# Normalising feed-forward rows two steps ahead, and scoring layer 1's first pair among the last feed-forward steps

## The chip, the cores and the metric

One NeuronCore of one Trainium2 chip runs the whole program. The metric is device time in microseconds (us), the median of several executions. The engines are TensorE (PE in the views, PEld for its weight loads), VectorE (DVE), ScalarE (ACT), GpSimd (POOL) and the sync engine (SP), which issues the DMAs inside the attention layers. Each engine works through its own instruction stream in order and waits on semaphores where it needs another's result.

## The reference

The input x is 64 sequences of 64 channels by 256 positions, float32. It goes through four blocks, each added to x:

```
x = x + L0_xattn(layernorm(x), ctx)   # banded attention (|i-j| <= 64), 8 heads, relu gate, mix
x = x + L0_ffn(layernorm(x))          # out = (x @ weight) * scale, then a norm rule on each row:
                                      #   out *= tanh(n) / (n + 1e-7), out *= min(0.99 / |out|, 1)
x = x + L1_xattn(layernorm(x), ctx)   # full attention, 8 heads, rotary q and k
x = x + L1_ffn(layernorm(x))          # 4-bit weights with low-rank terms, relu, 256 -> 1024 -> 256
```

Both attentions need softmax over exp(score - row maximum), so a pair's row maxima come before its exponentials. A row of the layer-0 feed-forward is 256 values in and out; its sum of squares gives n.

## The kernel before

X stays in on-chip memory as 32 pairs of sequences, [128, 32, 256]. Everything runs pair by pair.

**Attention.** One `iteration(r)` of a layer works on several pairs at once, 16 heads each: it scores pair r+1 (`score_head`, TensorE line 451) for its row maxima (`maximum`, VectorE line 1157), forms the shifted scores of pair r (`shifted_head`, line 467) for the exponentials (`exp_head`, ScalarE line 757), and projects q and k of pair r+3. In layer 1 a projection (line 503) is followed by the rotary rows: ScalarE copies them with halves swapped (`turn_rows`, line 786, two activations each for q and k), VectorE multiplies (`rotate`, line 1185), GpSimd adds (`rot_sum`, lines 1368 and 1373), ScalarE rounds the high part (`high_part`, line 774) and GpSimd forms the two lower parts (`split`, lines 1353 to 1360). SP then lays the parts out and replicates them (`lay_out`, lines 359 and 362, `replicate`, lines 373 and 375); `score_head` waits for all of it on `stack_in`. GpSimd splits the row maxima (`split_max`, lines 1022 and 1024), TensorE turns them (`turn_max`, line 543), ScalarE copies them out (`max_out`, line 812), and SP writes them into the stacked rows (`shift_rows`, line 384), for which `shifted_head` waits. Iterations -3, -2 and -1 only fill this pipeline.

**Layer-0 feed-forward.** It has 36 steps, written out by hand. In step n VectorE normalises row pair n (`vector_apply` into `ff0_xn`, line 1132; the views call it ff_xn) and keeps the result of n-4 (`tensor_copy` into `ff`, line 1276). TensorE transposes pair n (line 658) and multiplies pair n-2 (line 672). ScalarE copies the transpose out (`ff0_xT`, line 939) and squares the product of n-2 with an accumulated sum (`junk`, line 945). Four product banks (1, 5, 3, 4) and two transpose banks (0, 2) are used in turn. Steps 0 to 7 stand beside the heads of layer 0's last iteration (`ff0_filling`). Steps 8 to 35 follow in `ff0_steps`, which calls `between(n)` ahead of each step. This `between` is each engine's list of what else is done there:

- the tail of layer 0's attention (n = 8 to 16);
- the feed-forward's gains for the first six pairs: `root` and `tanh` on ScalarE, `gain_norm` and `gain_clip` on VectorE (lines 1081 to 1102), six times `ff0_update` (line 1072 and the statistics in line 1029) at n = 12 to 14, the variance at n = 15, `vector_rstd` and the first `apply` of layer 1 at n = 17;
- layer 1's iteration -3 (TensorE n = 18, ScalarE 19 and 22, VectorE 20) and -2 (TensorE 23 and 30, ScalarE 24 and 31, VectorE 25), cut by heads.

After step 35 TensorE waits until VectorE has kept all 32 results (`f_keep`), because layer 1 scores into banks 0, 1 and 5 and its exponentials use 2 and 3. Only then does `run(-1)` start with iteration -1. VectorE does the gains of the other 26 pairs inside iteration -1 (`vector_within`) and updates X with them in iterations 0 to 9, two to five pairs in each.

The GpSimd and SP streams have no `between`: they start on layer 1 when layer 0 is done and wait for what they need. For SP the order in an iteration is side load, layout of pair r+2, maxima of pair r (second half), replication of pair r+2, maxima of pair r+1 (first half).

Of the kernel before, what the change touches and what calls it, by code (L numbers as in the profile page):

```python
# [15 lines left out]
PAIRS = BATCH // 2  # L16
HPP = 2 * HEADS
# [12 lines left out]
EARLY = PAIRS // X_CHUNKS  # L30
FF0_RING = 4
FF0_LAG = (2, 2, 4)
FIRST_CHUNK, SECOND_CHUNK = 6, 16
FILL = 8
SCORE_BANKS = 3
# [45 lines left out]
def build(nc, a, out):  # L81
# [12 lines left out]
    with stack:  # L94
# [186 lines left out]

        def ff0_turn_bank(n):

            return bank[2 if n > FILL and n % 2 else 0], n if n <= FILL else n - 1

        def ff0_bank(n):

            if n < FILL:
                return bank[(1, 5)[n % 2]], n - 1
            return bank[(1, 5, 3, 4)[n % 4]], n - 1 if n < FILL + 2 else n - FF0_RING + 1  # L290


# [348 lines left out]
        def _(e):  # L641
# [38 lines left out]
            def between(n):  # L680
                if n - FILL in tail:
                    tail[n - FILL]()
                if n == 18:
                    iteration(*early(-3))
                if n == 23:
                    iteration(*early(-2, range(0, 6)))
                if n == 30:
                    iteration(*early(-2, range(6, HPP)))

            ff0_steps(ff0, between)  # L690
            e.wait_ge(f_keep, PAIRS)
            run(-1)
            tail = next_tail

            def turn_chunk(c, cu):
# [222 lines left out]
        @block.scalar  # L918
        def _(e):
            e.dma_start(lora_in, a["lora_in"]).then_inc(lora_loaded, 16)  # L920
            e.dma_start(lora_out, a["lora_out"]).then_inc(lora_loaded, 16)
            e.dma_start(att_w[1][:, :, :], a["att_w1"]).then_inc(weights1_in, 16)
            e.dma_start(att_b[1][:, :], a["att_b1"]).then_inc(weights1_in, 16)
            e.wait_ge(cleared_s, 1)
            nc.scalar.activation(gain[:, 0:1], gain[:, 0:1], ACT.Sqrt).then_inc(table_in, 1)
            e.wait_ge(cleared_k, 1)
            e.dma_start(Ks[SHIFT_ROW:SHIFT_ROW + PARTS, :, :, :].rearrange("p a h t -> p (a h t)")
                        .bitcast(fp32), a["minus"]).then_inc(minus_in, 16)
            scalar_prepare(e, -AHEAD - 1)
            e.wait_ge(ln_var, 1)  # L930
            scalar_sqrt(0, EARLY)
            e.wait_ge(weights0_in, 2 * 16)

            def ff0(pair):
                n, u = num(pair, FF0_RING), pair[1]
                if active(pair, FF0_RING):
                    e.wait_ge(f_xT, n + 1)
                    wait_some(e, f_mm, n - FF0_RING + 1)
                    nc.scalar.activation(ff0_xT[:, u, :], ff0_turn_bank(n)[0][:, 0:T], ACT.Copy).then_inc(f_xTs, 1)
                late = at(pair, -FF0_LAG[1], FF0_RING)  # L940
                n, u = num(late, FF0_RING), late[1]
                if active(late, FF0_RING):
                    e.wait_ge(f_mm, n + 1)
                    wait_some(e, f_sq, n - 1)
                    nc.scalar.activation(junk[:, u % 2, :], ff0_bank(n)[0][:, 0:T], ACT.Square,
                                         accum_out=sumsq[:, bass.ds(n, 1)]).then_inc(f_sq, 1)

            _, run, tail = scalar_attention(e, 0, scalar_prepare, ff0_filling(ff0))
            run(-AHEAD)

            def root(chunk, first, end):
                e.wait_ge(f_sq, end)
                nc.scalar.activation(tmp[:, 0, first:end], sumsq[:, first:end], ACT.Sqrt).then_inc(f_root, 1)

            def tanh(chunk, first, end):
                e.wait_ge(f_norm, chunk + 1)
                nc.scalar.activation(tmp[:, 2, first:end], tmp[:, 1, first:end], ACT.Tanh).then_inc(f_tanh, 1)

            iteration, run, next_tail = scalar_attention(e, 1, scalar_edges)

            def between(n):
                if n - FILL in tail:
                    tail[n - FILL]()
                if n == 8:
                    root(0, 0, FIRST_CHUNK)
                if n == 10:
                    tanh(0, 0, FIRST_CHUNK)
                if n == 16:
                    e.wait_ge(ln_var, 4)
                    scalar_sqrt(0, FIRST_CHUNK)  # L970
                if n == 19:
                    iteration(*early(-3, range(0, 6)))
                if n == 22:
                    iteration(*early(-3, range(6, HPP)))
                if n == 24:
                    iteration(*early(-2, range(0, 6)))
                if n == 25:
                    e.wait_ge(ln_var, 5)
                    scalar_sqrt(TAIL_NORM, PAIRS)
                if n == 31:  # L980
                    iteration(*early(-2, range(6, HPP)))

            ff0_steps(ff0, between)
            root(1, FIRST_CHUNK, PAIRS)
            tanh(1, FIRST_CHUNK, PAIRS)
            run(-1, loop_from=4)
            tail = next_tail

            def turn_out(c, cu):
                e.wait_ge(g_xT, CHUNK * c + CHUNK)  # L990
                wait_some(e, g_up, HB * c - HB)
                for blk in range(2):
                    nc.scalar.activation(xT[:, cu, blk, :], bank[blk][:, :], ACT.Copy).then_inc(g_xTs, 1)

            def relu_chunk(c, cu, beside={}):
                wait_some(e, g_down, CHUNK * c - CHUNK)
                for hb in range(HB):
                    if hb in beside:
                        beside[hb]()
                    e.wait_ge(g_up, HB * c + hb + 1)  # L1000
                    nc.scalar.activation(hidden[cu][:, hb, :], bank[2 + hb % 2][:, :], ACT.Relu,  # L1001
                                         bias=up_b[:, hb:hb + 1]).then_inc(g_relu, 1)

            turn_out(0, 0)
            relu_chunk(0, 0, tail)
            turn_out(1, 1)
            e.wait_ge(ln_var, 9)
            scalar_sqrt(TAIL_NORM, PAIRS)
            relu_chunk(1, 1)
            with e.Fori(1, PAIRS // CHUNK // 2) as i:  # L1010
                turn_out(i * 2, 0)
                relu_chunk(i * 2, 0)
                turn_out(i * 2 + 1, 1)
                relu_chunk(i * 2 + 1, 1)
# [90 lines left out]
        def vector_within(e, n, h):  # L1105


            if n == -1 and h == 2:
                gain_norm(e, 1, FIRST_CHUNK, PAIRS)
            if n == -1 and h == 6:  # L1110
                gain_clip(e, 1, FIRST_CHUNK, PAIRS)
            if n in (0, 1) and h % 3 == 1 and h < 15:
                ff0_update(e, FIRST_CHUNK + 5 * n + h // 3)
            if n == 1 and h == 15:
                vector_var(e, FIRST_CHUNK, SECOND_CHUNK, ff_vec, SECOND_CHUNK + NORM_STEPS)
            if n == 2 and h == 1:
                vector_rstd(e, 6, FIRST_CHUNK, SECOND_CHUNK)
            if 2 <= n < 10 and h in (3, 11):
                ff0_update(e, SECOND_CHUNK + 2 * (n - 2) + h // 8)
            if n == 9 and h == 15:  # L1120
                vector_var(e, SECOND_CHUNK, PAIRS, ff_vec, PAIRS + 2 * NORM_STEPS)
            if n == 10 and h == 1:
                vector_rstd(e, 7, SECOND_CHUNK, PAIRS)
# [11 lines left out]
        def vector_attention(e, l, extra=None, within=None, beside=None):  # L1135
# [81 lines left out]
            if l == 0:  # L1217
                tail[6] = lambda: update(at(TAIL, -1))

            def iteration(r):  # L1220
                p1, p3, m1 = at(r, 1), at(r, AHEAD), at(r, -1)
                for h in range(HPP):
                    if within and isinstance(r[0], int):
                        within(e, num(r), h)
                    if h == 5:
# [29 lines left out]
        def _(e):  # L1255
# [7 lines left out]
            e.wait_ge(weights0_in, 2 * 16)  # L1263

            def ff0(pair):
                n, u = num(pair, FF0_RING), pair[1]
                if n == 0:
                    e.wait_ge(ffn_ready, PREP_BLOCKS)
                if active(pair, FF0_RING):
                    wait_some(e, f_xT, n - FF0_RING + 1)  # L1270
                    vector_apply(n, ff0_xn[:, u, :], f_xn)
                late = at(pair, -FF0_LAG[2], FF0_RING)
                n, u = num(late, FF0_RING), late[1]
                if active(late, FF0_RING):
# [10 lines left out]
            def between(n):  # L1285
# [15 lines left out]
                    iteration(*early(-3)[:1])  # L1301
                if n == 21:
                    vector_var(e, TAIL_NORM, PAIRS, ln_vec, PAIRS + NORM_STEPS)
                if n == 28:
                    vector_rstd(e, 5, TAIL_NORM, PAIRS)
                if n == 25:
                    iteration(*early(-2)[:1])

            ff0_steps(ff0, between)
            e.wait_ge(f_keep, PAIRS)  # L1310
            run(-1, loop_from=4)
            tail = next_tail

            def norm_chunk(c):
# [232 lines left out]
```

## Time and profile before

| | |
|---|---|
| median of 3 runs | 1329.06 us (1322.9 to 1331.28) |
| the profiled execution | 1333.56 us |
| its span, first to last instruction | 1331.8 us |
| mean granted TensorE clock | 0.982 of full speed |
| TensorE busy | 1263.2 us (95%) |
| VectorE busy | 909.1 us (68%) |
| ScalarE busy | 847.8 us (64%) |
| GpSimd busy | 676.6 us (51%) |

The profiled execution took 4.5 us more than the median of the runs. Times inside the span are counted from its first instruction. A row of a timeline gives start, duration, engine, line, operation and, in brackets, how long the engine had been idle and who released it. The granted clock is 1.00 at TensorE's upper level (2.4 GHz) and 0.50 at the lower (1.2 GHz).

### The profile page before, as it was taken

How to read it: one execution, taken by the hardware profiler on the slowest of the kernel's cores; microseconds unless marked ns; L12 is line 12 of the kernel's file. 1: busy time of each engine (PE TensorE's matmuls, PEld its weight loads, DVE VectorE, ACT ScalarE, POOL GpSimd, SP SyncE). 2: the span in 40 equal slices, each digit the busy share in tenths (PEclk: the TensorE clock that was granted, in tenths of full speed). 3: DMA queues.
4: the chain of work that ended last, by engine and by line, in shares of the span. 5: the costliest groups of instructions: out<-in, count | busy, mean ns of one | idle time of the engine just before them, and what ended most of it. 6: DMA issues, size and time to landing. Idle time of an engine off the chain costs nothing.

```text
span 1331.8 us, 35495 instructions
## 1 busy us (share of the span) xinstructions
PE 1263.2 (95%) x11100; PEld 839.9 (63%) x11100; DVE 909.1 (68%) x1924; ACT 847.8 (64%) x1849; POOL 676.6 (51%) x1169
## 2 busy tenths in 40 slices
PE   6999999999999998778899999999999989999998
PEld 3666667667776765454565656666666546666665
DVE  6778778888887875569999978888888842111110
ACT  2567677776777776556888788888888763222111
POOL 4577778787878865045455445555555211000000
PEclk9999999999999999888999999999999999999999
DMA  8554454544444440034344434444444300000000
GB/s 206 120 131 107 114 117 111 116 110 118 113 114 117 99 92 7 13 67 102 89 107 96 97 90 103 105 112 97 103 108 108 86 2 16 16 16 16 16 16 32
DMA packets 90486, 113.34 MB, mean 85 GB/s; under 512 B 13971, under 2 KB 80275, under 8 KB 82739
## 3 DMA queue, kind: packets, MB, share of 16 engines
q1 hardware_dynamic: 89216, 111.25, 35.9%
q10 hardware_dynamic: 1206, 1.29, 0.3%
q8 instruction: 34, 0.56, 0.2%
q14 instruction: 30, 0.25, 0.1%
HBM read 18.66 MB, written 4.19 MB: 17 GB/s over the span
## 4 chain that ended last, share of the span: by engine, by line
PE 73%; DVE 10%; POOL 6%; issue 4%; ACT 3%; DMA 2%; SPq 1%; POOLq 0%; ACTq 0%; DVEq 0%
PE bank L491 13%; PE bank L451 12%; PE bank L467 12%; PE bank L721 8%; PE bank L712 8%; PE bank L449 5%; DVE row_max L1157 5%; PE bank L503 4%; POOL probs L1386 4%; PE bank L672 2%; PE bank L522 2%; PE bank L555 2%; PE bank L532 1%; PE bank L543 1%; DVE stats L1029 1%
## 5 line engine op out<-in xcount | busy, mean ns | idle before, releaser
L1157 DVE TENSOR_REDUCE row_max<-bank 128x2 f32<-128x384 f32 (+1 forms) x1024 | 598.5, 617 | 107.0 <-PE bank L451 102.8
L757 ACT ACTIVATE probs<-bank 128x384 f32<-128x384 f32 (+1 forms) x1024 | 536.8, 542 | 165.1 <-PE bank L467 154.8
L451 PE MATMUL bank<-Ks,Qs 96*128 96x192 bf16 (+1 forms) x2048 | 371.4, 263 | 10.9 <-DVE row_max L1157 9.7
L467 PE MATMUL bank<-Qs,Ks 128*128 128x192 bf16 (+1 forms) x2048 | 366.3, 261 | 13.9 <-ACT probs L757 11.1
L1386 POOL TENSOR_SCALAR_AFFINE_SELECT probs<-probs 128x256 f32<-128x256 f32 (+1 forms) x512 | 259.1, 530 | 105.9 <-ACT probs L757 85.5
L451 PEld LDWEIGHTS bank<-Ks,Qs 96*128 96x128 bf16 x2048 | 186.4, 98 | 121.1 <-DVE row_max L1157 39.7
L491 PE MATMUL bank<-probs,V 128*32 128x192 f32 (+1 forms) x4096 | 248.0, 360 | 4.7 <-POOL probs L1386 3.4
L467 PEld LDWEIGHTS bank<-Qs,Ks 128*128 128x128 bf16 x2048 | 186.7, 98 | 45.4 <-ACT probs L757 28.7
L449 PE MATMUL bank<-band,ident 128*128 128x384 bf16 x512 | 168.8, 330 | 2.5 <-DMA Ks<-Ks 2.0
L491 PEld LDWEIGHTS bank<-probs,V 128*32 128x32 f32 x4096 | 107.3, 109 | 84.5 <-issue 40.5
L1323 DVE TENSOR_TENSOR X<-bank,X 128x256 f32 (+1 forms) x32 | 13.6, 425 | 185.6 <-PE bank L721 185.6
L712 PE MATMUL bank<-Ks,ffn_w 128*128 128x512 f32 x256 | 111.8, 593 | 0.0
L1459 POOL TENSOR_TENSOR X<-X,down_b 128x256 f32 x32 | 23.1, 750 | 169.5 <-DVE xn L1132 169.5
L1368 POOL TENSOR_TENSOR rot<-rot,rope 128x256 f32<-128x256 f32 x64 | 46.7, 730 | 117.7 <-ACT rot L786 117.7
L712 PEld LDWEIGHTS bank<-Ks,ffn_w 128*128 128x128 f32 x256 | 48.4, 190 | 56.8 <-issue 56.4
L1001 ACT ACTIVATE probs<-bank,up_b 128x512 f32<-128x512 f32 x32 | 22.0, 687 | 85.7 <-PE bank L712 85.7
L1001 ACT ACTIVATE Qs<-bank,up_b 128x512 f32<-128x512 f32 x32 | 22.0, 687 | 76.1 <-PE bank L712 76.1
L449 PEld LDWEIGHTS bank<-band,ident 128*128 128x128 bf16 x512 | 49.4, 96 | 32.0 <-issue 15.6
L1357 POOL TENSOR_SCALAR Qp<-q_rest 128x256 bf16<-128x256 f32 x64 | 54.3, 848 | 27.3 <-DVE q_rest L1167 21.9
L503 PE MATMUL bank<-xn,att_w 128*128 128x256 f32 x192 | 63.9, 418 | 1.8 <-DVE xn L1132 1.6
L1022 POOL TENSOR_TENSOR row_max<-row_max 128x16 f32<-128x16 f32 x64 | 13.8, 215 | 100.7 <-DVE row_max L1157 100.7
L786 ACT ACTIVATE rot<-bank,att_b 64x256 f32<-64x256 f32 x128 | 60.0, 469 | 3.4 <-PE bank L503 0.3
(114 smaller groups left out, 1625.2 us busy)
## 6 DMA issues: line engine op xcount, KB each, us to landing
Ks<-Ks SPq DMA_DIRECT2D x64, 576.0 KB
Qs<-Qs SPq DMA_DIRECT2D x128, 192.0 KB
Qs<-Qp SPq DMA_DIRECT2D x192, 64.0 KB
Ks<-Kp SPq DMA_DIRECT2D x192, 64.0 KB
X<-in_x SPq DMA_DIRECT2D x4, 1024.0 KB, 13.8
side<-in_ctx_crossed SPq DMA_DIRECT2D x32, 128.0 KB, 2.1
side<-in_ctx SPq DMA_DIRECT2D x32, 128.0 KB, 2.1
out<-X SPq DMA_DIRECT2D x8, 512.0 KB, 3.0
```

Source lines behind the costliest of these rows:

```text
L449: nc.tensor.matmul(dst[:, 0:2 * win], ident16[:, :], band16[:, :], start=True, stop=False)
L451: last = nc.tensor.matmul(dst[:, blk * win:(blk + 1) * win], Qs[0:SHIFT_ROW, pair[1], h, blk * P:(blk + 1) * P], Ks[0:SHIFT_ROW, pair[1], ...
L467: last = nc.tensor.matmul(dst[:, blk * win:(blk + 1) * win], Ks[:, pair[1], h, blk * P:(blk + 1) * P], Qs[:, pair[1], h, start(blk):start( ...
L491: last = nc.tensor.matmul(dst[32 * j:32 * j + 32, first:first + win], V[:, pair[1], column:column + 32], probs[:, head % 8, blk * win:(blk ...
L503: nc.tensor.matmul(job_bank[b][:, 0:T], w[:, weight, :], source, start=True, stop=True).then_inc(s[f"{b}_filled"], 1)
L712: last = nc.tensor.matmul(bank[2 + hb % 2][:, :], up_w[:, blk, hb * P:(hb + 1) * P], xT[:, cu, blk, :], start=(blk == 0), stop=(blk == 1))
L721: last = nc.tensor.matmul(bank[4 + j % 2][:, 0:T], hidden[cu][:, hb, j * P:(j + 1) * P], down_w[:, hb, :], start=(hb == 0), stop=(hb == HB ...
L757: nc.scalar.activation(probs[:, h % 8, 0:2 * win], exp_bank[h % 2][:, 0:2 * win], ACT.Exp, scale=SCALE).then_inc(s["exped"], 1)
L786: nc.scalar.activation(rot[here, 2 * n + 1, :], job_bank[bk][there, 0:T], ACT.Identity, bias=b[there, column:column + 1]).then_inc(s["turn ...
L1157: nc.vector.tensor_reduce(row_max[:, pair[1], h // HEADS, 0, h % HEADS * 2:h % HEADS * 2 + 2], bank_of(pair, h)[:, 0:2 * win].rearrange("p ...
L1357: nc.gpsimd.tensor_scalar(parts[:, u, 1, :], rest[:, :], 1.0, None, ALU.mult).then_inc(s[mid], 1)
L1386: return nc.gpsimd.affine_select(out=part, in_=part, compare_op=ALU.is_ge, fill=0.0, base=base, pattern=[[0, 4], [-sign, width]], channel_ ...
```

## The change

VectorE's part of the feed-forward runs two row pairs ahead: step 0 normalises pairs 0, 1 and 2, and step n pair n+2. The four buffers of `ff0_xn` are the same, so step n waits for the transpose of pair n-2 in place of n-4. The reciprocal for the last four pairs moves from n = 28 to n = 26, and ScalarE's square root for it from n = 25 to n = 23.

From pair 28 on the feed-forward uses three banks in place of six: transposes only bank 2, products banks 3 and 4 in turn. Banks 0, 1 and 5 are so free for scores. TensorE scores heads 0 to 2 of layer 1's pair 0 ahead of step 32 and heads 3 and 4 ahead of step 33, with the projection of pair 2's q at head 1; the rest of iteration -1 follows step 35, ahead of the wait for `f_keep`. VectorE takes maxima 0 and 1 ahead of step 33, 2 to 4 ahead of step 34 and 5 to 7 ahead of step 35, and the rest after the steps. ScalarE's part of iteration -1 follows its steps, with `tanh` in the middle of it, and VectorE's gains move from heads 2 and 6 to heads 8 and 14. GpSimd and SP are unchanged.

```diff
+FF0_LATE = 28
+FF0_AHEAD = 2
...
         def ff0_turn_bank(n):
 
+            if n >= FF0_LATE:
+                return bank[2], n
             return bank[2 if n > FILL and n % 2 else 0], n if n <= FILL else n - 1
...
                 return bank[(1, 5)[n % 2]], n - 1
+            if n >= FF0_LATE:
+                return bank[(3, 4)[n % 2]], n - 1
             return bank[(1, 5, 3, 4)[n % 4]], n - 1 if n < FILL + 2 else n - FF0_RING + 1
...
                     iteration(*early(-2, range(6, HPP)))
+                if n == 32:
+                    e.wait_ge(f_xTs, FF0_LATE)
+                    e.wait_ge(f_keep, FF0_LATE - 2)
+                    iteration(*early(-1, range(0, 3)))
+                if n == 33:
+                    iteration(*early(-1, range(3, 5)))
 
             ff0_steps(ff0, between)
+            iteration(*early(-1, range(5, HPP)))
             e.wait_ge(f_keep, PAIRS)
-            run(-1)
+            run(0)
...
-                if n == 25:
+                if n == 23:
                     e.wait_ge(ln_var, 5)
                     scalar_sqrt(TAIL_NORM, PAIRS)
...
             root(1, FIRST_CHUNK, PAIRS)
+            iteration(*early(-1, range(0, 9)))
             tanh(1, FIRST_CHUNK, PAIRS)
-            run(-1, loop_from=4)
+            iteration(*early(-1, range(9, HPP)))
+            run(0, loop_from=4)
...
-            if n == -1 and h == 2:
+            if n == -1 and h == 8:
                 gain_norm(e, 1, FIRST_CHUNK, PAIRS)
-            if n == -1 and h == 6:
+            if n == -1 and h == 14:
                 gain_clip(e, 1, FIRST_CHUNK, PAIRS)
...
             def ff0(pair):
-                n, u = num(pair, FF0_RING), pair[1]
+                n = num(pair, FF0_RING)
                 if n == 0:
                     e.wait_ge(ffn_ready, PREP_BLOCKS)
-                if active(pair, FF0_RING):
-                    wait_some(e, f_xT, n - FF0_RING + 1)
-                    vector_apply(n, ff0_xn[:, u, :], f_xn)
+                for step in range(FF0_AHEAD + 1) if n == 0 else (n + FF0_AHEAD,):
+                    if step < PAIRS:
+                        wait_some(e, f_xT, step - FF0_RING + 1)
+                        vector_apply(step, ff0_xn[:, step % FF0_RING, :], f_xn)
...
-                if n == 28:
+                if n == TAIL_NORM - FF0_AHEAD:
                     vector_rstd(e, 5, TAIL_NORM, PAIRS)
                 if n == 25:
                     iteration(*early(-2)[:1])
+                if n == 33:
+                    iteration(*early(-1, range(0, 2)))
+                if n == 34:
+                    iteration(*early(-1, range(2, 5)))
+                if n == 35:
+                    iteration(*early(-1, range(5, 8)))
 
             ff0_steps(ff0, between)
+            iteration(*early(-1, range(8, HPP)))
             e.wait_ge(f_keep, PAIRS)
-            run(-1, loop_from=4)
+            run(0, loop_from=4)
```

## Rows read from the trace of the kernel before

**Rows 1.** Busy time by stretch: window, us, PE, PEld, DVE, ACT, POOL, PEclk, DMA share, GB/s
```profile
534.00:563.00 29.00, 21.77 (x101) 14.62 (x94) 17.80 (x58) 13.04 (x40) 0.72 (x1) 0.82 0.05 14
563.00:592.00 29.00, 22.19 (x95) 17.70 (x93) 15.35 (x41) 16.86 (x59) 12.39 (x18) 0.82 0.25 53
592.00:608.00 16.00, 11.51 (x49) 5.19 (x50) 14.94 (x31) 5.60 (x13) 10.13 (x17) 0.65 0.47 104
...
900.00:1000.00 100.00, 99.83 (x1001) 64.82 (x1005) 86.40 (x158) 85.49 (x186) 53.88 (x95) 1.00 0.45 104
```

**Rows 2.** TensorE's waits, 534 to 592 us: us in total, times, longest
```profile
PE bank L658 <- DVE ff_xn L1132: 13.6, 6, 3.2
```

**Rows 3.** Timeline, all engines, around step 20
```profile
563.12 1.03 PE L672 MATMUL bank<-ff_w,ff_xT 128*128 128x256 f32 x4
...
563.60 1.95 ACT L786 ACTIVATE rot<-bank,att_b 64x256 f32<-64x256 f32 x4
...
566.37 0.81 DVE L1132 TENSOR_SCALAR ff_xn<-X,mean,rstd 128x256 f32<-128x256 f32 x1
...
567.17 0.72 POOL L1373 TENSOR_TENSOR k_rest<-rot 128x256 f32<-128x256 f32 x1
...
567.23 0.69 PE L658 MATMUL bank<-ident,ff_xn 128*128 128x128 f32 x2 [3.08 <-DVE ff_xn L1132]
...
567.71 1.91 PE L672 MATMUL bank<-ff_w,ff_xT 128*128 128x256 f32 x4
```

**Rows 4.** TensorE's timeline, an undisturbed step (27 and 28), and two windows
```profile
583.70 0.38 PE L658 MATMUL bank<-ident,ff_xn 128*128 128x128 f32 x2
583.91 1.03 PE L672 MATMUL bank<-ff_w,ff_xT 128*128 128x256 f32 x4
584.78 0.38 PE L658 MATMUL bank<-ident,ff_xn 128*128 128x128 f32 x2
...
567.00:573.00 6.00, 5.77 (x17) 4.66 (x18) 3.96 (x16) 2.40 (x9) 1.10 (x3) 0.50 0.01 1
...
580.00:583.00 3.00, 3.00 (x10) 2.44 (x10) 1.54 (x5) 1.18 (x4) 0.45 (x1) 0.50 0.79 152
```

**Rows 5.** VectorE's timeline, steps 11 to 17
```profile
540.36 0.41 DVE L1132 TENSOR_SCALAR ff_xn<-X,mean,rstd 128x256 f32<-128x256 f32 x1
...
541.02 0.47 DVE L1072 SCALAR_TENSOR_TENSOR X<-ff,gain,X 128x256 f32<-128x256 f32 x1
...
542.72 0.40 DVE L1132 TENSOR_SCALAR ff_xn<-X,mean,rstd 128x256 f32<-128x256 f32 x1
...
558.80 0.18 DVE L1051 RECIPROCAL rstd<-rstd 128x6 f32<-128x6 f32 x1
```

**Rows 6.** TensorE's timeline, steps 2 and 5 in layer 0's last iteration
```profile
518.12 0.45 PE L658 MATMUL bank<-ident,ff_xn 128*128 128x128 f32 x2 [1.07 <-DVE ff_xn L1132]
...
527.15 0.44 PE L658 MATMUL bank<-ident,ff_xn 128*128 128x128 f32 x2 [0.31 <-DVE ff_xn L1132]
```

**Rows 7.** Pair 0's way to its stacked rows: timeline of ACT and SP, one window
```profile
572.17 0.41 ACT L774 ACTIVATE Qp<-q_rest 128x256 bf16<-128x256 f32 x1
...
582.40 0.82 SPq L375 DMA_DIRECT2D Ks<-Ks  x1
...
587.00:588.00 1.00, 1.00 (x9) 0.97 (x8) 0.66 (x2) 0.66 (x3) 0.00 (x0) 1.00 0.39 82
```

**Rows 8.** Timeline, iteration -1: TensorE, ScalarE and VectorE
```profile
592.53 0.39 PE L451 MATMUL bank<-Ks,Qs 96*128 96x256 bf16 x2 [1.02 <-DVE ff L1276]
...
594.69 1.95 ACT L786 ACTIVATE rot<-bank,att_b 64x256 f32<-64x256 f32 x4
...
600.96 6.66 DVE L1157 TENSOR_REDUCE row_max<-bank 128x2 f32<-128x512 f32 x11
607.54 0.48 DVE L1072 SCALAR_TENSOR_TENSOR X<-ff,gain,X 128x256 f32<-128x256 f32 x1
```

More of the change, by code:

```diff
@@ L1218, in vector_attention, with iteration @@
                 tail[6] = lambda: update(at(TAIL, -1))
-            def iteration(r):
+            def iteration(r, heads=range(HPP)):
                 p1, p3, m1 = at(r, 1), at(r, AHEAD), at(r, -1)
-                for h in range(HPP):
+                for h in heads:
                     if within and isinstance(r[0], int):
```

## The prediction

> **What bounds the kernel now.** I read the table by stretch first. In layer 1's steady state TensorE is busy 99.83 of 100 us; in the feed-forward steps it is busy 21.8 of 29 us and again 22.2 of 29, at a mean granted clock of 0.82 [rows 1]. So the stretch from 534 to 592 us loses time in two ways. The list of TensorE's waits names the first: 13.6 us in six waits, all of the transposes for a normalised row pair [rows 2]. The timeline shows how one arises. At step 20 ScalarE spends 1.95 us on the rotary rows, VectorE waits for them, and only then normalises pair 20; TensorE has nothing from 564.15 to 567.23, 3.08 us [rows 3]. The second loss follows the first: after the wait the four matmuls of a product take 1.91 us in place of 1.03, and the window 567 to 573 has a granted clock of 0.50, the lower of the two levels [rows 3, 4]. An undisturbed step takes 1.08 us (transpose to transpose) [rows 4].
>
> From 592.5 on VectorE bounds: 14.94 of 16 us busy [rows 1], with layer 1's first score at 592.53 and the last maximum of pair 0 ending just before 607.54, 15.0 us later [rows 8]. From there the work is the same before and after the change, so I take 607.54 as the point to compare.
>
> **Part 1, two steps ahead.** It adds and removes no instruction, only the places change; the three first normalisations stand together in step 0, where TensorE needs only the first. The work by stage, with times as in this execution:
>
> *Layer 0's last iteration.* The waits of steps 2 and 5 (1.07 and 0.31 us [rows 6]) go, since those pairs were normalised earlier. I count 1.2.
>
> *Steps 8 to 17.* VectorE does its gains up to 540.36. From there it has work without a pause: six pairs of normalisation and copy (540.36 to 541.02, 0.66 each), six updates with statistics (541.02 to 542.72 is two, 0.85 each), two updates of layer 0's tail at the same 0.85, and seven small operations for the variance, some 0.8 [rows 5]. That is 3.9 + 5.1 + 1.7 + 0.8 = 11.5 us, so the reciprocal that was at 558.80 comes at about 551.9: 6.9 earlier. TensorE no longer sits behind it step by step: it may be two steps on. It needs 1.08 a step and some 2 us for the tail, under 9 us in all, so VectorE bounds here, not TensorE. TensorE's and ScalarE's earlier lag goes too: q and k of pair 0 are projected at about 552.5, and after steps 18 and 19 of 1.08 us ScalarE's rotary rows start at about 555.1 in place of 563.60 [rows 3], 8.5 earlier.
>
> *Steps 19 to 22.* The stall of 3.08 us shrinks to what ScalarE's 1.95 us leave, about 0.9, and the lower clock behind it (three steps at 2.1 in place of 1.08) goes. GpSimd's last sum for pair 0 ends 4.3 us after the rotary rows start (563.60 to 567.89 [rows 3]), so at 559.4. ScalarE's high part of q, which waited at 572.17 for its turn in the steps [rows 7], comes at about 559.1: 13.0 earlier.
>
> *Steps 23 to 31.* The stall ahead of step 25 goes the same way, with its lower clock (580 to 583 at 0.50 [rows 4]). With step 22 at 558.5, ten steps of 1.08, the projections (0.9 and 0.4) and 0.8 for ScalarE's rows TensorE is at step 32 at about 571.5.
>
> **Part 2, the early scores.** They need pair 0's stacked rows. Before, the last copy was issued at 582.40 and the transfers ran on to about 587.9 (82 GB/s still in the window to 588, of which the last part is mine to divide from the side load) [rows 7], 15.7 us after the high part. Nothing in that chain (GpSimd, SP, four dependent transfers) is changed, so it lands at T = 559.1 + 15.7 = 574.8. TensorE stands at step 32 from 571.5 and waits 3.3 us there, with products 30 and 31 queued behind the first score.
>
> Behind T the order costs something. VectorE's early maxima include the rotation of pair 2's q ahead of step 34, and ScalarE does those rows only after square 31 and `root`. At the lower level, which followed idle times of 3.08 and 3.24 us [rows 3, 4], three heads (0.43 each, twice the full-speed 0.2 per head of rows 8) and a projection (0.86) end at T + 2.2; a product is 0.86 at full speed, what a step of 1.08 leaves beside its transpose [rows 4], and 1.7 at half. Product 30 ends at 3.6, with the clock back on the way, heads 3 and 4 at 4.05, product 31 at 4.9, its square at 5.5, the root at 5.8, q's two rows (0.98 [rows 8]) at 6.75, and VectorE rotates at T + 6.85. It had finished maxima 0 to 2 and one copy at T + 3.55, so it waits 3.3 us. Its remaining work is that of before, 15.0 us from first score to last maximum [rows 8], and three copies that now lie within it, 1.0. The last maximum ends at T + 15.0 + 1.0 + 3.3 = T + 19.3 = 594.1, 13.5 us ahead of 607.5. With the 1.2 of the opening that is 14.7.
>
> Without part 2 the scores would start at the same T and end at T + 15.0, so I price part 2 by itself at +4.3 us. The bounds: -2 if the rows land early enough that maxima run beside the products, +6 if the clock stays low through both products.
>
> *Costs that no row shows.* The three banks: a late product waits for the copy of the one two before it. The cost lies between 0 and a whole step of 1.08 us for each of four steps, 4.3; I take 0, because the 3.3 us wait for T covers most of it. A normalisation beside GpSimd's work takes 0.81 in place of 0.41 [rows 3, 5]; VectorE has room where that happens, so between -0.5 and +1; I take 0. The clock between 541 and 552 us: TensorE has gaps of 1 to 1.5 us there, shorter than the ones that preceded a fall, but many. A fall would cost up to 2 us behind VectorE's bound; I take 1.0. The moved square root loads no table and the gains only trade places: 0.
>
> Sum: 14.7 - 1.0 = 13.7 us. The profiled execution, 1333.56, would become 1319.9; on the median, 4.5 lower, 1329.1 - 13.7 = **1315.4**.
>
> [...]
>
> **Rivals.** (a) *The early scores are free.* The rows land by 572 to 573, or TensorE comes late enough to find them there, and the maxima fill VectorE's gaps. Then part 2 costs nothing and part 1 gives its whole 19.0 less 1.0: 1329.1 - 18 = 1311. For it: VectorE is idle about half of steps 24 to 31 (15.35 busy of 29 [rows 1]). Against: T follows from the high part by a chain that I see at 15.7 us, and everything that TensorE gains makes it arrive earlier before T.
>
> (b) *Half the gain.* TensorE's waits for normalised rows are replaced by waits for VectorE's kept results or ScalarE's copies: both engines do the same 1.95 us of rotary rows, tanh and root in the same places. If each of the six waits keeps half its length and its lower clock, half of the 13.0 stays: 7.7 in all with the opening, less 1.0: 1322.4. For it: each wait in rows 2 has another busy engine behind it. Against: four buffers and banks let TensorE run two steps on.
>
> (c) *Slower.* The waits are cut into many short gaps, and the clock stays at the lower level through the steps. From step 13 (541.3) 19 steps at 2.14 us make 40.7, tail, projections and V at half speed 6.8; TensorE comes to step 32 at 588.8, where it was at about 589.5. Part 1 then gives 0.7 + 1.2 = 1.9, and part 2 costs its 4.3: 2.4 slower, 1331.5. It decides from the point where part 1 saves less than 4.3. Against it: from 583 to 589 the clock is full with this very pattern of steps.
>
> (d) *The ahead does not happen where it matters*, since the wait for the transpose of n-2 binds VectorE: then a pair is normalised one step ahead at most. TensorE transposes n-2 two steps before it is needed, so I see nothing for it; it would end near (b).
>
> **How the numbers follow.** My forecast 0.45, (a) 0.2, (b) with (d) 0.28, (c) 0.07. The range goes from 1306, a little under (a), to 1326, over (b), which leaves out (c) and the far ends. One per cent, about what a measurement can tell here, is 13.3 us: the bound is 1315.8, in the middle of my own case. So faster: half of 0.45 and all of (a), with a little of (b), 0.46; slower by over 1% needs 1342, beyond (c), 0.04; within 1% 0.50.
>
> **What would show it.** TensorE's waits for ff_xn fall from 13.6 to under 3 us; the reciprocal of 558.80 comes near 551; the high part of 572.17 near 558; one wait of 2 to 4 us at the first score of layer 1, released by a DMA; a wait of VectorE of about 3 us at line 1185 between maxima 2 and 3; the last maximum of pair 0 near 593. I am wrong if the first score finds its rows ready (a), if the waits for ff_xn turn into waits on line 1276 or 939 of the same length (b), or if the granted clock is 0.5 between 541 and 570 (c).

## The result, and the profile after

| | before | changed |
|---|---|---|
| median of 10 runs each | 1331.41 us | 1318.60 us |
| range of the runs | 1322.9 to 1333.66 | 1314.75 to 1320.99 |
| ratio | | 0.9916 (95% interval 0.9894 to 0.9937) |
| span of the profiled execution | 1331.8 us | 1313.0 us |

The change makes the kernel 0.6 to 1.1% faster, 12.8 us by the medians. The forecast was 1315.4, 13.7 faster than the 1329.1 of that time. Against the bound of 1% the result lies inside: 0.84%, with an interval that ends just beyond it.

The two profiled executions differ by 18.8 us, more than the runs do, and part of that has nothing to do with the change: 3.2 us lie ahead of the feed-forward and 1.8 behind the last mark below. The feed-forward's first transpose stands at 513.04 us before and at 509.83 after, although nothing ahead of it was changed. So I count from four marks within each execution: the first transpose (a), layer 0's last values group (b), layer 1's first score (c), and the sixth `ff0_update` of layer 1 (e), with the first of them (d) between.

| us | a to b | b to c | c to d | c to e | a to e |
|---|---|---|---|---|---|
| before | 20.52 | 58.97 | 15.01 | 31.18 | 110.67 |
| changed | 17.62 | 44.82 | 19.40 | 34.46 | 96.90 |

From a to e the changed kernel gains 13.8 us. In TensorE's waits of this stretch (512 to 600 us of the changed kernel) what was 13.6 us on normalised rows [rows 2] is 0.2:

```profile
PE bank L457 <- DMA Ks<-Ks: 3.1, 1, 3.1
PE bank L678 <- DVE ff L1292: 2.9, 2, 2.5
PE bank L664 <- ACT ff_xT L952: 1.7, 2, 0.9
...
PE bank L509 <- DVE xn L1147: 0.9, 1, 0.9
PE bank L664 <- DVE ff_xn L1147: 0.2, 1, 0.2
```

The first four rows are what came in its place, 8.6 us: the wait for pair 0's stacked rows, the waits for a kept result (line 1292), the short waits behind ScalarE's rotary rows, and one for layer 1's own normalised rows (xn). The stretches that answer to [rows 1], with the same columns:

```profile
534.00:563.00 29.00, 25.10 (x118) 17.54 (x118) 22.98 (x70) 18.17 (x60) 10.05 (x14) 0.94 0.09 24
563.00:592.00 29.00, 21.88 (x97) 13.36 (x96) 19.06 (x46) 11.95 (x37) 13.46 (x22) 0.74 0.49 104
```

In the first 29 us TensorE does 118 matmuls in place of 101, and the granted clock rises from 0.82 to 0.94. The second stretch holds the new wait and the low clock of iteration -1.

The timeline of the changed kernel shows three places. Step 11's product (step 11 multiplies pair 9) waits where nothing waited before; the rotary rows and the high part come early (551.44 and 555.62, which is 24.0 and 28.2 us after b; before, 563.60 and 572.17 [rows 3, 7] are 30.0 and 38.6 after b); and iteration -1 stops twice, TensorE at the first score and VectorE at the rotation:

```profile
534.57 0.42 DVE L1292 COPY ff<-bank 128x256 f32<-128x256 f32 x1
...
535.14 1.50 PE L678 MATMUL bank<-ff_w,ff_xT 128*128 128x256 f32 x4 [2.53 <-DVE ff L1292]
...
547.79 0.18 DVE L1066 RECIPROCAL rstd<-rstd 128x6 f32<-128x6 f32 x1
...
551.44 1.95 ACT L799 ACTIVATE rot<-bank,att_b 64x256 f32<-64x256 f32 x4
...
555.62 0.41 ACT L787 ACTIVATE Qp<-q_rest 128x256 bf16<-128x256 f32 x1
...
566.27 0.82 SPq L381 DMA_DIRECT2D Ks<-Ks  x1
...
572.27 0.38 PE L457 MATMUL bank<-Ks,Qs 96*128 96x256 bf16 x2 [3.10 <-DMA Ks<-Ks]
...
573.46 1.91 PE L678 MATMUL bank<-ff_w,ff_xT 128*128 128x256 f32 x4
...
579.15 0.48 DVE L1200 SCALAR_TENSOR_TENSOR rot<-bank,att_b,rope 128x256 f32<-128x256 f32 x1 [4.19 <-ACT rot L799]
```

### The profile page after: what moved, and what is told of

Read it like the earlier page. It is cut to its first block, busy times and chain, and to the rows that moved or that the text cites. A ratio compares the mean times of both kernels' runs of the same rounds, so it can differ in the third digit from the quotient of the medians.

```text
span 1313.0 us, 35495 instructions
## 1 busy us (share of the span) xinstructions
PE 1253.5 (95%) x11100; PEld 832.9 (63%) x11100; DVE 906.5 (69%) x1924; ACT 846.5 (64%) x1849; POOL 676.8 (52%) x1169
## 3 DMA queue, kind: packets, MB, share of 16 engines
HBM read 18.66 MB, written 4.19 MB: 17 GB/s over the span
## 4 chain that ended last, share of the span: by engine, by line
PE 44%; DVE 9%; ACT 2%; issue 2%; DMA 1%; SPq 0%; ACTq 0%; POOL 0%
PE bank L734 9%; PE bank L725 8%; PE bank L497 8%; PE bank L457 7%; PE bank L473 7%; DVE row_max L1172 5%; PE bank L509 2%; DVE X L1087 1%; DVE stats L1044 1%; PE bank L561 1%; PE bank L528 1%; DVE rot L1200 1%; PE bank L538 1%; ACT rot L799 1%; PE bank L549 1%
## 5 line engine op out<-in xcount | busy, mean ns | idle before, releaser
L1346 DVE TENSOR_TENSOR X<-bank,X 128x256 f32 (+1 forms) x32 | 13.6, 425 | 185.6 <-PE bank L734 185.6
L1037 POOL TENSOR_TENSOR row_max<-row_max 128x16 f32<-128x16 f32 x64 | 13.8, 215 | 100.6 <-DVE row_max L1172 100.6
## 6 DMA issues: line engine op xcount, KB each, us to landing
X<-in_x SPq DMA_DIRECT2D x4, 1024.0 KB, 13.8
```

## The experiments

Each was timed over 5 rounds beside the kernel before on the same chip. The intervals are read from each one's profiled execution.

| | ratio to before (95% interval) | median, us | b to c | c to d | c to e |
|---|---|---|---|---|---|
| e1, part 1 only | 0.9883 (0.9864 to 0.9902) | 1315.12 | 44.80 | 15.01 | 31.21 |
| e2, part 2 only | 1.0001 (0.9984 to 1.0018) | 1328.90 | 54.18 | 17.68 | 33.35 |
| e3, changed, rows ahead of step 33 | 0.9886 (0.9867 to 0.9906) | 1314.84 | 45.11 | 17.36 | 32.43 |
| e4, part 1, other product banks | 0.9868 (0.9848 to 0.9889) | 1312.36 | 43.28 | 14.99 | 31.20 |
| f1, the changed kernel again | 0.9913 (0.9886 to 0.9939) | 1316.32 | 44.76 | 17.48 | 32.54 |
| f2, changed with both repairs | 0.9878 (0.9853 to 0.9904) | 1312.55 | 42.80 | 17.85 | 32.91 |
| f3, e4 with one step ahead | 0.9923 (0.9896 to 0.9951) | 1318.45 | 49.64 | 15.01 | 31.23 |
| f4, e4 with three steps ahead | 0.9889 (0.9864 to 0.9914) | 1313.07 | 42.30 | 14.99 | 31.17 |

The kernel before had a median of 1329.16 beside e1 to e4 and 1329.12 beside f1 to f4.

**e1 and e2: each part alone.** e1 is the kernel before with VectorE's new `ff0`, the reciprocal at n = 26 and the root at n = 23; the banks and `run(-1)` stay. e2 is the changed kernel with

```diff
-FF0_AHEAD = 2
+FF0_AHEAD = 0
```

> Only the rows two steps ahead; banks and iteration -1 as before. Theory A (part 1 gives all of the gain and part 2 takes some of it back): layer 1's first score about 14 us earlier than before, counted from the last values group of layer 0 (59.0 us there before, 44.8 in the changed kernel), and 15.0 us from the first score to the first update of X in layer 1 (19.4 in the changed kernel), so 4 us faster than the changed kernel: a ratio to before of 0.987 to 0.989. Rival B (the early scores are needed for the gain): the ratio is 0.993 to 0.996, slower than the changed kernel.

> Only the three banks and the early scores; no row is normalised ahead. Theory A: the rows of pair 0 have landed when TensorE comes to step 32, so no wait on the DMA, but VectorE still waits some 3 us for the rotary rows of pair 2; net 0 to +3 us against before, ratio 1.000 to 1.003. Rival B: 4 to 6 us faster than before, ratio 0.995 to 0.997.

e1 has the same 44.8 us from b to c as the changed kernel and the 15.0 of before from c to d; it is 0.3% faster than the changed kernel in the ratio, at the edge of what the intervals tell apart (0.9883 and 0.9916), and in the profile 3.3 us shorter from c to e. So part 1 carries the whole gain. e2 is no change at all in the runs. Its profile shows no wait on the DMA, and the wait of 2.5 us for the rotary rows:

```profile
590.48 0.48 DVE L1200 SCALAR_TENSOR_TENSOR rot<-bank,att_b,rope 128x256 f32<-128x256 f32 x1 [2.52 <-ACT rot L799]
```

e2's first score comes 4.8 us earlier after b than before's. It gives 2.2 us back up to e, and the runs don't show the remaining 2.6: their interval allows a gain of 2.1 us at most. Why they don't stays open.

**e3: is it the order on ScalarE that blocks VectorE?**

```diff
+                if n == 33:
+                    iteration(*early(-1, range(0, 3)))
 
             ff0_steps(ff0, between)
             root(1, FIRST_CHUNK, PAIRS)
-            iteration(*early(-1, range(0, 9)))
+            iteration(*early(-1, range(3, 9)))
```

> The changed kernel, with ScalarE's part of heads 0 to 2 of iteration -1 (the rotary rows of pair 2's q) ahead of its step 33, in place of behind square 31 and the root. Theory A: VectorE's wait of 4.2 us at the rotation shrinks to 1 to 2, first score to first update 16.5 to 17.5 us in place of 19.4, 2 to 3 us faster than the changed kernel, ratio 0.989 to 0.991. Rival (VectorE's wait only covers a wait for the last products and kept results, which bound anyway): the wait moves to line 1292 and the interval stays at 19 us or more.

VectorE's wait at the rotation falls from 4.19 to 2.01 us and c to d from 19.40 to 17.36. The first row is e3's product 30:

```profile
574.38 1.92 PE L678 MATMUL bank<-ff_w,ff_xT 128*128 128x256 f32 x4
...
577.83 0.48 DVE L1202 SCALAR_TENSOR_TENSOR rot<-bank,att_b,rope 128x256 f32<-128x256 f32 x1 [2.01 <-ACT rot L799]
```

That looked like the whole answer until f1.

**f1: the changed kernel again.**

> The changed kernel once more, beside the others of this group: ratio to before 0.990 to 0.993; 44 to 45.5 us from the last values group of layer 0 to layer 1's first score, 19.4 from there to the first update of X in layer 1.

b to c came out as expected, but c to d is 17.48, not 19.40, with nothing edited. TensorE waited for the same transfer about as long in both (3.27 and 3.10 us); the clock after it was not the same. These are the five microseconds from the first score, of the changed kernel first, then of f1 (granted clock third from the end):

```profile
572.00:577.00 5.00, 4.73 (x20) 3.65 (x21) 2.27 (x4) 0.47 (x2) 1.51 (x2) 0.66 0.34 78
```

```profile
571.00:576.00 5.00, 4.07 (x24) 3.14 (x24) 2.28 (x4) 1.58 (x6) 1.49 (x2) 1.00 0.36 80
```

The next two rows are f1's, a product at full clock (1.91 us in the changed kernel above) and the wait of VectorE:

```profile
572.47 1.03 PE L678 MATMUL bank<-ff_w,ff_xT 128*128 128x256 f32 x4
...
576.59 0.48 DVE L1200 SCALAR_TENSOR_TENSOR rot<-bank,att_b,rope 128x256 f32<-128x256 f32 x1 [2.52 <-ACT rot L799]
```

Square 31, which the rotary rows stand behind, depends on products 30 and 31, so the clock sets VectorE's wait: 2.5 us at the upper level, 4.2 at the lower. e3 had the lower level (its product took 1.92 us), so its 2.01 must be held against the 4.19; f2 below, which has the same edit, waited 1.94 us with a product of 1.84. The order on ScalarE is part of the cause, worth about 2 us at the lower clock. At the upper clock it wasn't measured.

**e4: the wait ahead of product 9.** In both kernels product 9 uses bank 5, as product 7 did. `ff0_bank` therefore returns n - 1 as the count of kept results for n = 8 and 9, so that product 9 waits until result 7 is kept, which VectorE does in step 11, behind `gain_clip` and with it `tanh`. From step 8 on banks 3 and 4 are free, so e4 starts with them:

```diff
-            return bank[(1, 5, 3, 4)[n % 4]], n - 1 if n < FILL + 2 else n - FF0_RING + 1
+            return bank[(3, 4, 1, 5)[n % 4]], n - FF0_RING + 1
```

> Part 1 alone, and from step 8 on the products go through banks 3, 4, 1, 5 in place of 1, 5, 3, 4, so that product 9 does not wait for the result of product 7. Theory A (the wait of 2.5 us ahead of product 9, and the lower clock behind it, are what held part 1 under its forecast): that wait goes, the granted clock stays at 1.00 from 534 to 545 us, and the interval from the last values group to the first score is 2 to 3 us shorter than in part 1 alone; 2 to 3 us faster than it. Rival C (VectorE's own queue bounds there): the wait goes, VectorE's gains run through, and the first score moves by less than 0.7 us.

The wait goes. From 534 to 546 us the clock is 1.00 where the changed kernel had 0.86, and VectorE is busy 11.49 of 12 us in place of 9.66. Of e4 first, then of the changed kernel:

```profile
534.00:546.00 12.00, 10.07 (x52) 5.96 (x49) 11.49 (x39) 7.37 (x25) 0.77 (x1) 1.00 0.00 0
```

```profile
534.00:546.00 12.00, 10.70 (x48) 6.96 (x48) 9.66 (x33) 6.02 (x19) 0.73 (x1) 0.86 0.00 0
```

The first score comes 1.5 us earlier than in e1, between theory A (2 to 3) and rival C (under 0.7). With the wait gone VectorE's own queue bounds: from the end of `gain_clip` to the reciprocal it takes 546.50 - 534.99 = 11.5 us, without a pause. That is the 11.5 of the prediction. TensorE now waits for it there, 1.9 us for ff_xn in two places. e4 is the fastest version by ratio, but its interval overlaps those of e1, f2 and f4: that the other banks save time is shown in the profile (1.5 us to the first score) and not in the runs.

**f2: both repairs in the changed kernel** (e3's edit, e4's banks, and `e.wait_ge(f_keep, FF0_LATE)` ahead of the early scores).

> The changed kernel with both repairs: products through banks 3, 4, 1, 5, and ScalarE's rotary rows of pair 2's q ahead of its step 33. Theory A: 43.3 us to the first score and 17.4 from there to the first update, so 3.5 us faster than the changed kernel and still 2.4 slower than part 1 with the product banks (e4), ratio 0.988 to 0.990. Rival B (the early scores pay once nothing blocks them): as fast as e4 or faster, ratio 0.987 or less.

Its intervals came within 0.5 us of theory A (42.8 and 17.9), but its ratio lies just between the two forecasts, and the runs put it beside e4 and f4: 0.9878, 0.9868 and 0.9889 can't be told apart, nor can the medians. Part of the reason stands at the other end. From the first to the sixth `ff0_update` the versions with the early scores take 15.1 us (f2: 590.75 to 605.81) and those without 16.2 (e4: 586.46 to 602.67). These are e4's rotation and second update, then f2's:

```profile
589.30 0.48 DVE L1186 SCALAR_TENSOR_TENSOR rot<-bank,att_b,rope 128x256 f32<-128x256 f32 x1 [0.62 <-ACT rot L787]
...
590.30 0.91 DVE L1073 SCALAR_TENSOR_TENSOR X<-ff,gain,X 128x256 f32<-128x256 f32 x1
```

```profile
592.79 0.47 DVE L1202 SCALAR_TENSOR_TENSOR rot<-bank,att_b,rope 128x256 f32<-128x256 f32 x1
...
593.78 0.57 DVE L1089 SCALAR_TENSOR_TENSOR X<-ff,gain,X 128x256 f32<-128x256 f32 x1
```

f2 has neither the wait of 0.62 us for ScalarE's rotary rows nor the long update, and so 1.1 us comes back. TensorE is further ahead when VectorE reaches the updates (first shifted head 2.5 us before them in f2, 1.1 in e4); that the later place of the gains is what gives it that lead is my reading, and no run tests it. Measured up to e the early scores cost 1.3 us (f1 against e1) to 3.3 (the changed kernel against e1).

**f3 and f4: how long a lead.** e4 with `FF0_AHEAD` at 1 and at 3.

> e4 with one step ahead in place of two. If the lead has to cover ScalarE's 1.95 us of rotary rows (two steps of 1.08), a wait of 0.5 to 1.5 us for ff_xn comes back at each of the two rotations, and the stretch where VectorE updates X stays bound by VectorE: 1 to 3 us longer to the first score than e4's 43.3, ratio 0.988 to 0.990. Rival: one step is enough (43.3 within 0.5), since the wait for the rotary rows binds ScalarE in any case.

> e4 with three steps ahead. VectorE then needs the transpose of n-1 before it normalises n+3 into the same buffer, so it waits for TensorE in turn. What bounds after e4 is VectorE's own queue and the way to the stacked rows, which a longer lead doesn't shorten: 43 to 44 us to the first score, within 1 us of e4. Rival: it is faster by 1 us or more, if the lead was still short.

One step is not enough, by more than I expected: 6.4 us more from b to c, and 8.2 us of waits for ff_xn in seven places. TensorE's waits in f3:

```profile
PE bank L659 <- DVE ff_xn L1133: 8.2, 7, 2.0
```

Each of the longer ones also costs clock, as before: around the rotary rows the transpose waits 2.01 us and the next takes 0.69 in place of 0.4:

```profile
554.40 0.44 PE L659 MATMUL bank<-ident,ff_xn 128*128 128x128 f32 x2 [2.01 <-DVE ff_xn L1133]
556.16 0.69 PE L659 MATMUL bank<-ident,ff_xn 128*128 128x128 f32 x2 [0.46 <-DVE ff_xn L1133]
```

Around the same rotary rows TensorE's wait was 3.08 us before [rows 3], 2.01 with one step, and 0.87 with two, where ScalarE's copy and no longer VectorE ends it. Each step of lead took off one step of 1.08 us, until another engine ended the wait. Three steps leave it as it is. Of the changed kernel, then of f4:

```profile
553.94 0.41 PE L664 MATMUL bank<-ident,ff_xn 128*128 128x128 f32 x2 [0.87 <-ACT ff_xT L952]
```

```profile
552.26 0.41 PE L659 MATMUL bank<-ident,ff_xn 128*128 128x128 f32 x2 [0.87 <-ACT ff_xT L940]
```

Three steps give 1.0 us from b to c and nothing in the runs. In VectorE's waits of f4 the new one is there as expected:

```profile
DVE ff_xn L1133 <- PE bank L659: 4.0, 4, 1.7
```

## Why the prediction was right

*The opening.* Forecast 1.2, measured 2.9 (a to b, 20.52 to 17.62). e2 still has the two waits of steps 2 and 5 (1.06 and 0.30 us) but a granted clock of 1.00 there, and takes 18.91. So the waits are worth 1.3, and the other 1.6 is clock: the execution of before had the lower level from 518.5 to 522 us, with this product behind the wait of 1.07 us [rows 6]:

```profile
518.40 1.89 PE L672 MATMUL bank<-ff_w,ff_xT 128*128 128x256 f32 x4
```

Those 1.6 us belong to that execution rather than to the kernel.

*Steps 8 to 17.* Forecast: the reciprocal 6.9 us earlier, bound by VectorE. Measured from b 4.9 (25.24 to 20.34). The term that I missed is the wait of product 9: the prediction lets TensorE run two steps on everywhere, where the code makes product 9 wait until result 7 is kept. It cost 2.5 us of TensorE, a stretch at the lower clock, and 1.96 us of VectorE, which waited for layer 0's mix. e4 takes it away, and VectorE's 11.5 us come out as worked: the reciprocal stands 18.3 us after b, as forecast.

*Steps 19 to 22.* Forecast from b: the high part 13.0 us earlier; measured 10.4 (38.61 to 28.17), 2.6 short. In e4 it is 12.4, so 2.0 of the 2.6 are product 9 and 0.6 stays unexplained. The short waits of 0.87 us behind ScalarE's rows are the 0.9 of the prediction. My 1.0 for the clock between 541 and 552 us was not needed for its own reason: in the changed kernel the one fall there came behind the 2.5 us wait, and e4, without that wait, had 1.00 throughout, with gaps of 0.8 to 1.1 us. But its premise, that gaps so short come before no fall, does not hold in general. The fall of before's opening stands behind waits of 0.89 and 1.07 us, and f4's in iteration -1 behind one of 0.86:

```profile
574.61 1.21 PE L452 MATMUL bank<-Ks,Qs 96*128 96x256 bf16 x4 [0.86 <-DVE row_max L1158]
...
575.00:576.00 1.00, 1.00 (x5) 0.74 (x5) 1.00 (x3) 0.42 (x1) 0.77 (x2) 0.50 0.78 126
```

*The way to the stacked rows.* Forecast 15.7 us from the high part to landing, measured 16.65 (555.62 to 572.27), and TensorE waited 3.10 where 3.3 was said. The chain took 0.4 us longer up to the issue of the last copy (10.65 against 10.23) and 0.5 longer behind it: the last copy was issued at 566.27 and the score came 6.0 us later, where the sum has 5.5. One thing differs there that the prediction does not count. SP issues the side load right behind the last copy, 0.9 us after it, where it was 5.2 before; these are the changed kernel's row, then the one of before:

```profile
567.13 0.53 SPq L349 DMA_DIRECT2D side<-in_ctx  x1
```

```profile
587.59 0.34 SPq L343 DMA_DIRECT2D side<-in_ctx  x1
```

Whether that load slows the copy was not tested.

*The price of part 2.* Forecast c to d 19.3, measured 19.40, with the lower clock that I assumed. VectorE rotates 6.88 us after the first score, where 6.85 was worked out; its wait was 4.19 in place of 3.3, since the maxima ahead of it were done earlier, and its other work 15.2 in place of 16.0. f1 shows that the 19.40 was one of two outcomes, 17.48 the other; and 1.1 us of it come back within five updates, since d was not the neutral point I took it for. My +4.3 was right for that execution at that mark. As the price of the edit it is 1.3 to 3.3. The three banks, put at 0, cost nothing that shows: behind 545 us TensorE has no wait for a kept result.

*The sum.* From a to e 13.8, and 12.2 without the clock of before's opening, against 14.7 worked out and 13.7 forecast. The errors were +1.7 (opening), -2.6 (steps 8 to 22, 2.0 of it product 9), -1.0 (transfers), -0.1 (c to d) and +1.1 (beyond d). They nearly cancel, and that is luck, as is the agreement with the 13.7, which carries 1.0 for a clock that did not fall that way. What held is the mechanism: the waits for normalised rows and the clock behind them are the gain, VectorE bounds steps 8 to 17, and the early scores cost more than they bring. Of the rivals, (a) falls by the 3.1 us wait, (b) and (d) by 0.2 us of waits for ff_xn (of the 13.6, 4.6 came back as the waits that (b) names, on lines 1292 and 952 here: a third) and by f4, where a longer lead does meet the wait for the transpose and gains nothing in the runs, and (c) by the clock of 0.94.

## What to carry to other kernels

A producer that works in lockstep beside a consumer passes on every detour that its queue makes. Each step of lead takes one step off the consumer's longest wait, until another engine's work ends that wait (here 3.08, 2.01 and 0.87 us with none, one and two steps of 1.08), and one step more leaves it as it is. When work is pulled forward past a transfer, look at what is queued behind it: here the last products, and through them the other engine's first piece of the same pulled-forward work. When a ring of banks changes use, see which of them is reused first; a one-line rotation of the order saved 1.5 us up to the first score in the profile, about what the early scores cost, though the runs cannot tell that much.

## What the hardware did that I had not expected

The same kernel, after the same wait of 3.1 to 3.3 us, had a granted clock of 0.66 over the next five microseconds in one execution and 1.00 in another, and the next 19 us differed by 1.9. One profile of a stretch with such a wait is a sample, not the cost: e3 against the changed kernel looked like a gain of 2.0 us, and the changed kernel against itself showed 1.9.
